# Attention inside an audio tower: probabilities turned by transposes, row sums divided out after the mix, rotations moved from ScalarE and GpSimd to VectorE

## The reference

```python
q = apply_rope(split_heads(x @ Wq)); k = apply_rope(split_heads(x @ Wk)); v = split_heads(x @ Wv)
sim = einsum('bid,bjd->bij', q, k) * scale          # causal mask, -inf above the diagonal
attn = softmax(sim, axis=-1)
out = einsum('bij,bjd->bid', attn, v)               # heads joined again
h = h + out @ Wo + bo
# apply_rope: pairs (x1, x2) of neighbouring features become
#   (x1 * cos - x2 * sin, x1 * sin + x2 * cos), angles by position
```

## Time and profile before

| what | value |
|---|---|
| median of 3 runs | 1788.51 us (1787.77 to 1788.92) |
| the profiled execution's own time | 1788.28 us |
| its span | 1786.5 us |
| PE, PEld, DVE, ACT, POOL busy | 85%, 81%, 70%, 56%, 57% of the span |
| attention stage | from about 89.6 to 860 us, first `turn` at 118.90 us |

### The profile page before, as it was taken

How to read it: one execution, slowest core, us unless ns; L and a number is a source line. 1 busy time by engine, 2 the same in 40 slices (tenths; PEclk the granted TensorE clock), 3 DMA queues, 4 the chain that set the end, 5 groups by cost and what they waited for, 6 DMA issues and landing times. The chain is left out here.

```text
span 1786.5 us, 31373 instructions
## 1 busy us (share of the span) xinstructions
PE 1525.2 (85%) x11301; PEld 1440.1 (81%) x11301; DVE 1250.3 (70%) x2526; ACT 995.8 (56%) x2138; POOL 1019.2 (57%) x814
## 2 busy tenths in 40 slices
PE   5389999999999999999499999999998937689129
PEld 4279999999999998998399999999987836688029
DVE  6547676868677877776346766666678569559896
ACT  4547575657575757665355555455544434459552
POOL 4479586969687777864466767766765633000000
PEclk8679999999999999999699999999999968899569
DMA  6490000000001001000465555555554331003313
GB/s 237 147 300 19 18 19 25 31 25 30 25 14 38 13 22 33 4 31 10 154 177 143 144 136 146 135 147 140 140 136 107 71 96 35 18 1 130 104 52 113
DMA packets 86129, 150.44 MB, mean 84 GB/s; under 512 B 7992, under 2 KB 63608, under 8 KB 85720
## 3 DMA queue, kind: packets, MB, share of 16 engines
q1 hardware_dynamic: 75464, 134.62, 24.6%
q0 software_dynamic: 10512, 13.83, 4.6%
HBM read 111.88 MB, written 49.91 MB: 91 GB/s over the span
## 5 line engine op out<-in xcount | busy, mean ns | idle before, releaser
L1534 POOL TENSOR_TENSOR expert_w_low<-expert_raw,expert_w_high 128x768 fp32r<-128x768 f32 x152 | 288.3, 1946 | 170.3 <-ACT expert_w_high L1359 164.3
L835 ACT ACTIVATE expert_raw<-psum,neg_max 120x376 f32<-120x376 f32 (+2 forms) x384 | 176.0, 479 | 99.3 <-DVE neg_max L996 99.2
L664 PE MATMUL psum<-diag,expert_raw 128*128 128x128 f32 (+2 forms) x1536 | 198.9, 279 | 8.2 <-DVE diag L1005 7.3
L1012 DVE TENSOR_TENSOR pt_low<-psum,pt_high 128x752 fp32r<-128x752 f32 x128 | 120.5, 941 | 118.1 <-ACT pt_high L844 118.1
L1506 DVE TENSOR_TENSOR expert_act_low<-expert_act,expert_act_high 128x384 fp32r<-128x384 f32 x152 | 140.1, 921 | 80.0 <-ACT expert_act_high L1397 79.4
L664 PEld LDWEIGHTS psum<-diag,expert_raw 128*128 128x128 f32 (+2 forms) x1536 | 180.3, 190 | 17.9 <-DVE diag L1005 11.2
L1397 ACT ACTIVATE expert_act_high<-expert_act 128x384 fp32r<-128x384 f32 x152 | 79.8, 525 | 204.7 <-DVE expert_act L1501 203.5
L1318 PE MATMUL psum<-slots_high,expert_w_high 128*128 128x384 f32 x608 | 160.1, 344 | 16.6 <-DVE expert_act L1501 15.4
L936 POOL TENSOR_TENSOR qk_low<-rotated,qk_high 128x376 fp32r<-128x376 f32 x128 | 144.1, 1126 | 47.1 <-ACT qk_high L828 44.3
L959 POOL TENSOR_TENSOR rotated<-expert_raw 128x376 f32<-128x376 f32 x128 | 127.9, 1000 | 56.8 <-ACT expert_raw L822 42.6
L1318 PE MATMUL psum<-slots_low,expert_w_high 128*128 128x384 f32 x608 | 156.4, 338 | 0.0
(11 more groups left out here) (296 smaller groups left out, 4422.6 us busy)
## 6 DMA issues: line engine op xcount, KB each, us to landing
expert_raw<-in_experts SPq DMA_DIRECT2D x152, 384.0 KB, 3.1
x_slots<-in_c_slots SPq DMA_DIRECT2D x4, 3168.0 KB, 29.4
slot_rows<-x_slots SPq DMA_DIRECT2D x19, 396.0 KB, 4.6
up_spill<-held SPq DMA_DIRECT2D x5, 1128.0 KB, 5.0
held<-up_spill SPq DMA_DIRECT2D x5, 1128.0 KB, 5.7
attn_x<-tok_xt SPq DMA_DIRECT2D x6, 752.0 KB, 4.0
x_parts<-attn_x SPq DMA_DIRECT2D x6, 752.0 KB, 4.6
patch<-in_patches SPq DMA_DIRECT2D x8, 376.0 KB, 7.0
```

The lines of the kernel that those rows point to most:

```text
L664: last = pe.matmul(psum[0:nj, BANK_PT + bank, at:at + ni], probs[0:ni, h % 2, src:src + nj], diag[0:ni, h % 2, it, 0:ni], start=True, stop ...
L835: last = act.activation(probs[0:ni, h % 2, at:at + P * it + ni], score_bank(h % 2, it), ACT.Exp, bias=neg_max[0:ni, h % 2, it:it + 1], acc ...
L1012: dve.tensor_tensor(pt[1][:, h % 2, :, :], psum[:, BANK_PT:BANK_PT + 2, 0:TOK], pt[0][:, h % 2, :, :].bitcast(F32), ALU.subtract).then_inc ...
L1534: pool.tensor_tensor(w[1][:, g % RING, :], raw[:, g % RAW, :], w[0][:, g % RING, :].bitcast(F32), ALU.subtract).then_inc(w_low, 1)
```

## The change

The six matmuls with diagonal matrices of `turn` become six transposes against one identity. The probabilities are then not divided by their sums. Instead `inverses` (DVE) makes the reciprocals of a whole pair at once, `spread_inverses` (ACT) spreads each over 64 columns, three more transposes on PE turn them (two with the second `turn` of a pair, one with its first `mix`), `keep_inverse` and `scale_out` (DVE) copy them out of PSUM, and `scale_out` multiplies the mixed output by them, in PSUM.

`raw_copy` on ACT is gone: `swap_pairs` reads PSUM and, in the same place, DVE multiplies by the cosines. POOL keeps the sine product, the sum and the low part. `swapped` and `rotated` have four buffers in place of two. `out_high` and `out_low` of a pair move into the next step: behind `turned_high` and `turned_low` of its first head. For the last pair of a batch they stay at the step's end.

```diff
-RAW_CHUNKS, EARLY_CHUNKS = 4, 2
+RAW_CHUNKS, EARLY_CHUNKS, AHEAD_ROWS = 4, 2, 4
...
                 def turn(b, h):
-                    pe.wait_ge(diag_made, 16 * b + h + 1)
+                    pe.wait_ge(exp_made, 16 * b + h + 1 + CR_EXP)
                     pe.wait_ge(pt_ready, 16 * b + h + CR_PT)
+                    if h % 2 == 0 and 16 * b + h:
+                        pe.wait_ge(inv_kept, 2 * (8 * b + h // 2) - 1)
...
-                            last = pe.matmul(psum[0:nj, BANK_PT + bank, at:at + ni],
-                                             probs[0:ni, h % 2, src:src + nj],
-                                             diag[0:ni, h % 2, it, 0:ni], start=True, stop=True)
+                            last = pe.transpose(psum[0:nj, BANK_PT + bank, at:at + ni],
+                                                probs[0:ni, h % 2, src:src + nj], ident[0:ni, 0:ni])
+                    if h % 2:
+                        pe.wait_ge(inv_spread, 8 * b + h // 2 + 1)
+                        last = turn_inverse(b, h // 2, (0, 1))
                     last.then_inc(turned, 1)
...
-                def raw_copy(b, n):
-                    act.wait_ge(proj_made, 16 * b + n + 1)
-                    act.wait_ge(rot_made, 16 * b + n + 1)
-                    act.activation(raw[:, n % 2, :], psum[:, BANK_PROJ, 0:TOK], ACT.Copy).then_inc(raw_made, 1)
...
+                def spread_inverses(b, c):
+                    act.wait_ge(inv_made, 8 * b + c + 1)
+                    act.activation(inv_wide[:, c % 2, :, :].rearrange("p t (u n) -> p u t n", u=2),
+                                   inv_sum[:, c % 2, :, :].rearrange("p u (t o) -> p u t o", o=1)
+                                   .broadcast_to((P, 2, TILES, HEAD)), ACT.Copy).then_inc(inv_spread, 1)
...
                 def swap_pairs(b, n):
-                    dve.wait_ge(raw_made, 16 * b + n + 1 + CR_RAW)
+                    m, k = 16 * b + n, n % AHEAD_ROWS
+                    dve.wait_ge(proj_made, m + 1)
+                    if m >= AHEAD_ROWS:
+                        dve.wait_ge(rot_made, m - AHEAD_ROWS + 1 + CR_ROT)
+                        dve.wait_ge(qk_ready, m - AHEAD_ROWS + 1 + CR_QK)
                     dve.memset(holder[:, n % (2 * PAIRS):n % (2 * PAIRS) + 1], 0.0)
-                    dve.stream_shuffle(swapped[:, n % 2, :], raw[:, n % 2, :], swap).then_inc(swap_made, 1)
+                    dve.stream_shuffle(swapped[:, k, :], psum[:, BANK_PROJ, 0:TOK], swap).then_inc(swap_made, 1)
+                    dve.tensor_tensor(rotated[:, k, :], psum[:, BANK_PROJ, 0:TOK], cos[:], ALU.mult).then_inc(cos_made, 1)
...
+                def keep_inverse(b, c):
+                    dve.tensor_copy(inv_rows[:, 0:2 * P].rearrange("p (t n) -> p t n", t=2),
+                                    psum[:, BANK_PT:BANK_PT + 2, TOK:TOK + P]).then_inc(inv_kept, 1)
+
+                def scale_out(b, c):
+                    dve.wait_ge(mixed, 16 * b + 2 * c + 2 + CR_MIX)
+                    dve.tensor_copy(inv_rows[:, 2 * P:TOK], turned_inverse(2)).then_inc(inv_kept, 1)
+                    dve.wait_ge(inv_kept, 2 * (8 * b + c + 1))
+                    dve.tensor_tensor(psum[:, BANK_O, 0:TOK], psum[:, BANK_O, 0:TOK], inv_rows[:], ALU.mult).then_inc(o_scaled, 1)
```

More of the change, by code:

```diff
@@ L448, in attention @@
         qk = [sb(f"qk_{part}", [P, 2, 2, TOK], F32R) for part in ("high", "low")]
-        raw, swapped = (shared[:, 2 * TOK * i:2 * TOK * (i + 1)].rearrange("p (u n) -> p u n", u=2) for i in range(2))
-        rotated = sb("rotated", [P, 2, TOK])
+        swapped = shared[:, 0:AHEAD_ROWS * TOK].rearrange("p (u n) -> p u n", u=AHEAD_ROWS)
+        rotated = sb("rotated", [P, AHEAD_ROWS, TOK])
         cos = shared[:, 4 * TOK:5 * TOK]
@@ L663, in turn, with turn_inverse @@
                             at, src = col + P * (it - j), PROBS_AT[it] + P * j
-                            last = pe.matmul(psum[0:nj, BANK_PT + bank, at:at + ni],
-                                             probs[0:ni, h % 2, src:src + nj],
-                                             diag[0:ni, h % 2, it, 0:ni], start=True, stop=True)
-                    last.then_inc(turned, 1)
+                            last = pe.transpose(psum[0:nj, BANK_PT + bank, at:at + ni],
[3 more added lines that the diff above has]
+                        last = turn_inverse(b, h // 2, (0, 1))
+                    last.then_inc(turned, 1)
+                def turn_inverse(b, c, tiles):
+                    for it in tiles:
+                        ni = TILE_ROWS[it]
+                        last = pe.transpose(turned_inverse(it), inv_wide[0:ni, c % 2, it, :], ident[0:ni, 0:ni])
+                    return last
                 def mix(b, h):
@@ L1158, in step @@
                     turned_low(b, 2 * c)
+                    if c:
+                        out_low(b, c - 1)
                     if projects:
@@ L1183, in _ @@
                 maxima(0, 0)
-                diagonals(0, 0)
-                diagonals(0, 1)
+                inverses(0, 0)
                 for b in range(BATCH):
```

77 lines of the change are left out of this document (40 added, 37 removed).

## The result

| | before | after |
|---|---|---|
| median of 5 runs | 1788.51 us (1786.85 to 1790.35) | 1779.48 us (1777.33 to 1783.45) |
| profiled execution | 1788.28 us | 1777.33 us (span 1775.5) |

The ratio is 0.9952, interval 0.9937 to 0.9967: 9.0 us faster, where 13.9 were forecast. The profiled execution is the fastest of its five.

What follows compares the result with a forecast made beforehand. PE bounds the kernel before, the ring of ACT and DVE after. From 1788.3 us: batches 2 to 6 -12.0, batch 1 -0.2, batch 0 -2.6, batch 7 -1.5, start +2.4, sum -13.9: 1774 us, range 1753 to 1796.

Steps and rivals of the forecast that it cites:

- the ring of ACT and DVE: Attention step: ACT and DVE wait for each other in turn; 8.15 us before, 8.73 after, longer than PE's 8.04.
- PE's part: PE's own work per attention step: loses two turns of 1.30 us, gets 15 transposes, 1.65 us; 8.99 becomes 8.04.
- Steps 0 to 6 of a full batch: Attention steps with their routing extras: 10.1, 9.2, 9.2, 9.1, 9.1, 10.1 and 8.7, together 65.5 us, from 67.6.
- step 5: Attention step with the logits: they delay the second turn by 1.0 us and `odds_exp` adds 0.38; 10.1 us.
- Step 7 with the begin: Last step of a batch with the next batch's begin: 26.0 us, from 26.32.
- batches 2 to 6: Full batches of the attention stage: 2.4 us saved each, 12.0 in all.
- batch 0: First batch, bare steps: 6 x 0.26 + 0.7 (step 0) + 0.3, 2.6 us saved.
- Start: Ahead of the first turn: PE waits 1.0 for shuffle and product in place of 0.48, five times; +2.4 us.
- the end of batch 7: End of the last batch: uncovered scaling takes 0.8 us from the batch's saving of 2.3, leaving 1.5.
- Rival 2: DVE's list bounds the attention stage, new PSUM operations costing more than their rows: slower, 1795 us; chance 0.16.
- Rival 4: PE's clock falls in one attention step in ten as PE idles and transposes: 42 us, 1819; chance 0.03.

Runs made afterwards that it cites:

- e3: The changed kernel with each of the three transposes of reciprocals in a step issued twice; 1783.62 us.
- e6: The changed kernel with PE's wait for the projection's bank, from the second batch on, only in steps with routing work and step 7; 1778.89 us.
- e12: The changed kernel with the second unit's shuffle and cosine product ahead of the reciprocals on DVE; 1783.41 us.
- e7: The changed kernel with e6's edit and the first unit's shuffle and product behind the maxima on DVE, except steps 3 to 5 of later batches; 1773.16 us.
- e11: e10 with the second unit's shuffle and cosine product ahead of the reciprocals on DVE; 1722.85 us.
- e4: The changed kernel with the output of the last batch's second-to-last pair split early, in its own step as before the change; 1776.19 us.
- e2: The kernel before with only the rotations changed (swaps and cosine products on DVE out of PSUM), turns still by diagonal matrices; 1797.51 us.
- e5: e2 with the second unit's swap and cosine product ahead of the second diagonal on DVE; 1788.47 us.
- e8: The change without its rotations part (raw copy and GpSimd's cosine product kept), first unit's shuffle behind the maxima, with e4's edit; 1750.05 us.
- e10: e8 with the second unit of each pair rotated by DVE straight from PSUM, the first still by raw copy; 1749.53 us.

## Why the prediction was right, and where not

- **The bound moves from PE to the ring of ACT and DVE: shown.** The ring was put at 8.73 and is 8.75. More work on PE (e3) hardly counts, PE's waits can be removed without gain (e6, and e12 in the bare steps), and two operations taken out of the ring shorten the step to 8.28 (e7). ACT waits 2.71 us for the maxima in the step, where some 3.0 were forecast.
- **PE's part: right.** Six transposes and the start of the next projection are 0.60 apart in e11 (142.59 to 143.19), where six at the forecast's 0.11 make 0.66; the whole step is 7.92 there, not 8.04. Its waits were forecast wrong: not `pt_low` but the new product delays it most (14.3 and 8.6 us in the list of waits, 9.5 for `pt_low`).
- **Steps 0 to 6 of a full batch: 65.4 measured along the ring, 65.5 forecast, and step for step.** From high part to high part they are 10.07, 9.22, 9.24, 9.10, 9.12, 9.86 and 8.74. Only step 5 is off, 0.24 too long: ACT waits 0.88 for the late turn and `odds_exp` adds 0.10, where 1.0 and 0.38 stood. From turn to turn step 0 looks shorter (9.43) and step 3 longer (9.61), because the turns of steps 1 to 3 are made while ACT still scales rows. In step 3 the transposes of the routing wait 0.57 us for the first unit's product, which I had missed when I listed who waits behind it, but ACT has no wait for PE in that step, so it costs nothing.

```profile
421.21 0.54 PE L732 MATMUL psum<-ident,x_rows 128*128 128x128 f32 x3 [0.57 <-DVE rotated L1014]
```

- **Step 7 with the begin:** 26.4 (26.7 in two batches) and not 26.0. So batches 2 to 6 gave 11.0 in place of 12.0, batch 0 1.9 in place of 2.6.
- **Start:** five waits of 1.11 to 1.24 for 0.57 to 0.63, and 31.81 us in place of 29.28 from the first projection to the first turn: +2.5 where +2.4 stood. In the profiled execution the stage itself began 2.9 us earlier, a difference between executions that hides it.
- **The step that failed is the end of batch 7.** "Less 0.8 at its end, where nothing covers the scaling": it is 5.1. (Steps 0 to 6 of this batch gave 1.65 of the 2.3; its step 5 has the first fall of the clock.) The low part of pair 6 now stands in step 7 on DVE behind the low part of the turn, and that behind the router's choice. PE waits 3.75 us for it and the clock falls. e4 takes back 3.3 by the medians and 3.7 by the trace.
- **The total.** Term by term the traces give -11.0 - 0.1 - 1.9 + 3.4 + 2.5 = -7.1 where the forecast had -13.9; 4.9 of the difference is batch 7. The medians say -9.0. The 1.9 us between lie within the spread of the executions (1777.33 to 1783.45), so that the total came as near as it did is in part luck.
- **Rival 2, operands in PSUM:** not borne out. The shuffle out of PSUM takes 0.59 (0.58 from SBUF before), the cosine product 0.53, the scaling from PSUM to PSUM 0.56, the copies of 256 and 120 columns 0.41 and 0.27. The Trainium skill, "VectorE: DVE Perf Modes", section "The TRN2 errata", would have made the shuffle 0.065 us longer (an estimate from its figures); the measurement, 0.006 us on the means (583 and 589 ns), decides against it here.
- **Rival 4, the clock:** not borne out in batches 0 to 6, where it is 1.00 in spite of 15 transposes a step, but it is not empty. In batch 7 it fell twice for 3.4 us, and e12 and e7 show that a wait of 0.66 us ahead of the logits, or of 2.22 ahead of a turn, can be followed by such a fall, at 1.5 to 1.6 us of time each. The sum of this rival is 1816 by its own terms, 1774 + 42, and not 1819; nothing hangs on it. The Trainium skill, "TensorE: Matmul & The Clock Gate", section "Part 4: PE-mode transpose", says that transposes do not count as busy for the clock in the way that matmuls do. The traces agree as far as they go: the three kernels that turn by matmuls (before, e2, e5) have no fall in the stage until its last output products are made, and of the eleven with transposes all but e8, e10 and e11 have one or more. No run changes this alone, and the transposes also leave PE idle for longer, which would be a cause of its own.
- **What the forecast did not ask:** which half brings the gain. By its own sums the raw copy saves 0.36 and the product costs 0.45, so the rotations' part was a loss of 0.09 in a bare step (measured 8.75 against 8.66), and with the start and the later batches it is 11.6 us.

## What to carry to other kernels

Where two in-order engines hand work back and forth, sum their starts around the ring before an edit is priced: what lies in the ring costs its full length, what lies in a wait inside it costs nothing, so one and the same shift of a shuffle and a product gave 27 us in one kernel (e11) and not 0.01 us of a bare step in another (e12). Split a change that has several parts and time each, since a gain can hide a loss of half its size. Measure a step along the chain that sets it, and where the same step is longer in some batches only, look at the granted clock before the order of instructions is blamed. When an operation is postponed by one step, look at the last step apart, where nothing follows that would hide it.

## What the runs showed of the hardware

DVE and GpSimd hold each other up where DVE's product has both operands in SBUF. In e5 the same product took 0.56 us while GpSimd was idle and 1.33 beside it:

```profile
137.03 0.56 DVE L998 TENSOR_TENSOR diag<-ident,inv_sum 128x384 f32<-128x384 f32 x1
...
138.65 1.33 DVE L998 TENSOR_TENSOR diag<-ident,inv_sum 128x384 f32<-128x384 f32 x1
```

GpSimd in the same time:

```profile
138.59 0.98 POOL L925 TENSOR_TENSOR qk_low<-rotated,qk_high 128x376 fp32r<-128x376 f32 x1 [2.58 <-ACT qk_high L822]
139.53 1.32 POOL L947 TENSOR_TENSOR expert_raw<-expert_raw,rope_sin 128x376 f32<-128x376 f32 x1
140.99 1.00 POOL L950 TENSOR_TENSOR rotated<-rotated,expert_raw 128x376 f32<-128x376 f32 x1
```

GpSimd was there 0.06 us earlier and kept its length, DVE ended 0.41 after it, and then GpSimd's next took 0.33 more than usual. The counts agree that the second to start is the one that pays. In e5, all 61 products that began while GpSimd made a low part were long (1.33 at the median); in e2, where GpSimd's low part began 0.24 us behind the product in 63 of 128 cases, every product took 0.56 and those low parts took 1.16 to 1.18 in place of 0.99. It looks as if one waits for the other to end; that is my reading, and no run tested it by itself. DVE's operations with an operand in PSUM kept their length beside GpSimd (the low parts, mean 0.94 in both kernels), and so did the shuffle with its one operand in SBUF. The diagonals had a mean of 0.91 in the kernel before, and 55 of the 128 were long. The forecast, which counted PE's instructions, did not have this; I take it for a part of the turns' gain, which is argued and not measured.
